# Third layer's end unrolled: attention parts first, norms behind them, inverses by node, skip rows made with K, V and Q

## The reference

```python
# third layer (H = 8 heads of DH = 16)
x_aug = concat([x, type_emb[node_types]], axis=-1)
K, Q, V = x_aug @ Wk, x_aug @ Wq, x_aug @ Wv
attn = einsum('ehd,ehd->eh', Q[dst], K[src]) * rel_scale[rel] / sqrt(DH)
attn_exp = exp(attn - max(attn))
attn_norm = attn_exp / (segment_sum(attn_exp, dst)[dst] + 1e-16)
out = segment_sum(attn_norm * V[src], dst) @ Wo + bo
h = out + x_aug @ Wskip
h = elu((h - mean(h)) * rsqrt(var(h) + 1e-5) * gamma + beta)
x = layernorm(x + h)
# fourth layer, its first part
C = 0.5 * (cos(edge_weight * pi / 10) + 1)          # one number per edge, the cutoff
W = (ssp(edge_attr @ mlp_w1.T + mlp_b1) @ mlp_w2.T + mlp_b2) * C
msg = (x @ lin1_w.T)[src] * W
```

## Time and profile before

| | |
|---|---|
| median of 3 runs | 9314.26 us (9308.85 to 9314.34) |
| profiled execution, its time | 9289.43 us |
| its span | 9287.6 us |
| busy: GpSimd, TensorE, VectorE, ScalarE | 66%, 57%, 53%, 19% |
| from the end of the third layer's loop to the first gather of the fourth | 6652.74 to 7105.95 us |

### The profile page before, as it was taken

One profiled execution on the slowest core, in us unless ns is written; L12 is line 12 of the kernel. 1 busy time (PEld: TensorE's weight loads), 2 busy tenths in 40 slices (PEclk: granted clock), 3 DMA queues, 4 the chain that ended last, 5 costly groups with the idle time before them and its releaser, 6 DMA issues. The chain is left out here.

```text
span 9287.6 us, 88604 instructions
## 1 busy us (share of the span) xinstructions
PE 5336.4 (57%) x27633; PEld 4325.2 (47%) x27633; DVE 4895.6 (53%) x10581; ACT 1745.2 (19%) x2599; POOL 6125.4 (66%) x6479
## 2 busy tenths in 40 slices
PE   4555555553344444444466666666435888887884
PEld 3444444442233333333355555555423555555553
DVE  5666666656422222222477777777654554555555
ACT  0000000002100000000300000000013555555553
POOL 5777777770377777777277777777403777777772
PEclk6666666665555555555677777777656878888886
DMA  5433434430233333333255555555301222222221
GB/s 172 115 114 111 115 110 115 113 105 2 57 77 77 75 77 76 75 77 75 84 166 164 164 165 164 164 164 164 91 1 52 73 74 74 72 74 72 74 73 36
DMA packets 391598, 906.48 MB, mean 98 GB/s; under 512 B 134405, under 2 KB 202936, under 8 KB 368288
## 3 DMA queue, kind: packets, MB, share of 16 engines
q0 software_dynamic: 232704, 538.22, 22.7%
q1 hardware_dynamic: 153538, 351.59, 12.6%
q10 hardware_dynamic: 4896, 11.01, 0.3%
HBM read 867.89 MB, written 32.45 MB: 97 GB/s over the span
## 5 line engine op out<-in xcount | busy, mean ns | idle before, releaser
L2117 POOL DMA_INDIRECT TMP<-schnet_table,src_idx x1616 | 1535.3, 950 | 964.1 <-issue 491.9
L1631 POOL DMA_INDIRECT PM<-hgt_kv_table,src_idx x1616 | 1528.0, 946 | 640.5 <-issue 467.0
L634 POOL DMA_INDIRECT PM<-gat_table,src_idx x1616 | 1531.8, 948 | 546.1 <-issue 492.2
L1177 POOL DMA_INDIRECT PM<-gcn_table,src_idx x1004 | 950.6, 947 | 306.0 <-issue 304.4
L1177 POOL DMA_INDIRECT TMP<-gcn_table,src_idx x612 | 577.3, 943 | 550.5 <-POOLq L1038 364.3
L1205 PE MATMUL ps<-TMP,PM 128*128 128x128 f32 x2008 | 515.5, 438 | 702.5 <-DMA PM<-gcn_table,src_idx 702.3
L1252 DVE TENSOR_TENSOR AC<-AC,ps 128x128 f32 x101 | 29.1, 288 | 1522.2 <-PE ps L1205 1522.2
L679 PE MATMUL ps<-PM 128*128 128x139 f32 x3232 | 781.2, 433 | 66.8 <-DVE PM L773 66.5
L1205 PEld LDWEIGHTS ps<-TMP,PM 128*128 128x128 f32 x2008 | 443.7, 325 | 763.8 <-DMA PM<-gcn_table,src_idx 626.9
L679 PEld LDWEIGHTS ps<-PM 128*128 128x128 f32 x3232 | 739.4, 327 | 73.1 <-DVE PM L773 72.8
L2144 PE MATMUL ps<-PM 128*128 128x128 f32 x3232 | 542.4, 321 | 362.6 <-issue 206.3
(11 more groups left out here) (383 smaller groups left out, 9008.2 us busy)
## 6 DMA issues: line engine op xcount, KB each, us to landing
PM<-local_dst_row SPq DMA_DIRECT2D x101, 1024.0 KB
PM<-local_dst_row SPq DMA_DIRECT2D x202, 512.0 KB, 3.9
PM<-in_attrT SPq DMA_DIRECT2D x101, 400.0 KB
xT<-in_rel_row SPq DMA_DIRECT2D x101, 384.0 KB, 4.8
PM<-gat_table,src_idx POOLq DMA_INDIRECT x1616
PM<-hgt_kv_table,src_idx POOLq DMA_INDIRECT x1616, 3.0
TMP<-schnet_table,src_idx POOLq DMA_INDIRECT x1616, 2.5
PM<-gcn_table,src_idx POOLq DMA_INDIRECT x1004, 2.5
```

Source lines behind the costliest of these rows:

```text
L634: pool.indirect_dma_start(out=g[:, par, t, 0:TAB0], out_offset=None, in_=tab0_d, in_offset=bass.IndirectOffsetOnAxis(ap=src_idx[:, i * ROU ...
L1177: pool.indirect_dma_start(out=g[n % DEEP][:, k, :], out_offset=None, in_=tab1_d, in_offset=bass.IndirectOffsetOnAxis(ap=src_idx[:, n * KT ...
L1631: pool.indirect_dma_start(out=g[:, par, t, 0:2 * P], out_offset=None, in_=kv_d, in_offset=bass.IndirectOffsetOnAxis(ap=src_idx[:, i * ROUN ...
L2117: pool.indirect_dma_start(out=g[:, b, k, :], out_offset=None, in_=tab3_d, in_offset=bass.IndirectOffsetOnAxis(ap=src_idx[:, (i * SLOTS + b ...
```

## The change

Second layer's loop: the type table for the skip part joins those of K, V, Q (t8, T8b now 512 columns wide), with the output bias added; one more load. Second layer's end: products 512 columns wide; the last 128, the skip rows, are copied by node into `skip`, which lies in xT. Third layer's loop: SP issues ten loads for what comes after, ahead of its own. Third layer's end: the rolled loop and the two blocks behind it become one unrolled block in BATCHES. The sums by head and the reference are turned to nodes, the inverse is taken by node (8 numbers), spread by ScalarE, turned back and multiplied in; products with output weights; skip rows added. This is done for all batches, then the norms follow. The cutoff is made on GpSimd as 1 - sin^2 with Sin on ScalarE; the row table is made group by group. Lines that are only moved are left out.

```diff
-        T8b = WA[0:TY, 0:3 * P // 2].bitcast(BF16)
+        T8b = WA[0:TY, 0:2 * P].bitcast(BF16)
...
+                sp.dma_start(out_bias, a["L2_gnn_bo"].partition_broadcast(NTYPE)).then_inc(hp_ld, 16)
...
-                    s.mark(dve.tensor_copy(T8s, PS[3][0:NTYPE, 0, 3 * P:4 * P]))
-                    s.link(dve.tensor_copy(t8, PS[3][0:NTYPE, 0, 0:3 * P]))
+                    s.mark(dve.tensor_copy(t8[:, 0:3 * P], PS[3][0:NTYPE, 0, 0:3 * P]))
+                    s.link(dve.tensor_tensor(t8[:, 3 * P:4 * P], PS[3][0:NTYPE, 0, 3 * P:4 * P], out_bias, ALU.add))
...
-                        nc.tensor.matmul(ps, xT[:, t_ * P:(t_ + 1) * P], WB[:, 0:3 * P], start=True, stop=False, skip_group_check=True)
+                        nc.tensor.matmul(ps, xT[:, t_ * P:(t_ + 1) * P], WB[:, 0:4 * P], start=True, stop=False, skip_group_check=True)
...
+                            nc.scalar.copy(skip[:, t_, :], PS[2 + t_ % 4 // 2][:, t_ % 2, 3 * P:4 * P]).then_inc(ev_act, 1)
...
+                            dve.tensor_copy(skip[:, t_, :], PS[2 + t_ % 4 // 2][:, t_ % 2, 3 * P:4 * P]).then_inc(ev_dve, 1)
...
+                for dst_, src_ in ((gamma, row_bc("L2_gnn_gamma")), (beta, row_bc("L2_gnn_beta")), (lin1, a["L3_gnn_lin1_w_T"]), (w1, a["L3_gnn_mlp_w1_T"]),
+                                   (w2, a["L3_gnn_mlp_w2_T"]), (lin2, a["L3_gnn_lin2_w_T"]), (linw, a["L3_gnn_lin_w_T"]), (b1, col_in("L3_gnn_mlp_b1")),
+                                   (l2b, col_in("L3_gnn_lin2_b")), (brow, a["L3_gnn_mlp_b2"].rearrange("(o f) -> o f", o=1))):
+                    sp.dma_start(dst_, src_).then_inc(late, 16)
                 either(sp, program)
+                sp.wait_ge(late, 160)
...
+            @block.gpsimd
+            def _(pool):
+                s = Steps(pool, cd)
+                pool.wait_ge(w_ld, 16)
+                s.link(pool.tensor_scalar(wk, cw, 0.05, None, ALU.mult))
+                s.link(pool.tensor_copy(wq, wk))
+                s.link(pool.tensor_scalar(wq, wq, -20.0, None, ALU.mult))
+                s.link(pool.tensor_tensor(wq, wq, cw, ALU.add))
+                pool.wait_ge(cs, 1)
+                s.link(pool.tensor_tensor(wq, wq, wq, ALU.mult))
+                s.link(pool.tensor_scalar(cw, wq, -1.0, 1.0, ALU.mult, ALU.add))
...
+                def turn_inverse(n):
+                    pe.wait_ge(wide, n + 1)
+                    if n >= 2:
+                        pe.wait_ge(num_ready, n - 1)
+                    for k, t_ in enumerate(tiles_of(n)):
+                        m = nc.tensor.transpose(group_ps(4 + n % 2, n)[:, k, :], y[:, t_, :], ident[:, :])
+                    m.then_inc(turned_r, 1)
+                def products(n):
+                    pe.wait_ge(num_ready, n + 1)
...
+                    for k, t_ in enumerate(tiles_of(n)):
+                        m = nc.tensor.matmul(group_ps(6 + n % 2, n)[:, k, :], acc2[:, 0, t_ * P:(t_ + 1) * P], WB[:, 4 * P:5 * P], start=True, stop=True)
+                    m.then_inc(out_mm, 1)
...
+                act.wait_ge(aged, 5)
+                nc.scalar.activation(age, age, ACT.Exp).then_inc(age_exp, 1)
+                for j in range(3):
+                    spread_inverse(j)
+                for j in range(3):
+                    rstds(j, 0)
+                exps(0)
+                exps(1)
+                rstds(0, 1)
+                norm(0)
+                finish(*BATCHES[0])
+                act.wait_ge(cd, 4)
+                nc.scalar.activation(wq, wq, ACT.Sin, scale=float(np.pi) / 20).then_inc(cs, 1)
+                exps(2)
+                rstds(1, 1)
+                norm(1)
+                finish(*BATCHES[1])
+                rstds(2, 1)
+                norm(2)
+                finish(*BATCHES[2])
...
+                def attended(j):
+                    def numerators(n):
+                        dve.wait_ge(turned_r, n + 1)
+                        num = acc2[:, 0, columns_of(n)].rearrange("p (k f) -> p k f", f=P)
+                        dve.tensor_tensor(num, num, group_ps(4 + n % 2, n), ALU.mult).then_inc(num_ready, 1)
+                    def with_skip(n):
+                        at = nodes_of(n)
+                        dve.wait_ge(out_mm, n + 1)
+                        dve.wait_ge(wide, BATCHES[j][1])
+                        dve.tensor_tensor(t[:, at, :], group_ps(6 + n % 2, n), skip[:, at, :], ALU.add).then_inc(out_read, 1)
+                    def stats(n):
+                        dve.wait_ge(out_read, n + 1)
+                        for t_ in tiles_of(n):
+                            s.mark(dve.bn_stats(out=st[:, t_, :], in_=t[:, t_, :]))
+                    lo, hi = BATCHES[j]
+                    for n in range(lo, hi + 2):
+                        if n < hi:
+                            numerators(n)
+                        if lo <= n - 1 < hi:
+                            with_skip(n - 1)
+                        if n - 2 >= lo:
+                            stats(n - 2)
+                    s.settle()
+                    variance(dve, s, st, w, span_of(BATCHES[j]))
+                    dve.sem_inc(var_ready[0], 1)
...
+                for j in range(3):
+                    inverses(j)
+                filter_bias()
+                attended(0)
+                attended(1)
+                attended(2)
+                first_norm(0)
+                first_norm(1)
+                residual(0)
+                first_norm(2)
+                residual(1)
+                scales(0)
+                residual(2)
+                scales(1)
+                scales(2)
```

More of the change, by code:

```diff
@@ new lines, in build, with sums_t @@
+        A = Arena(TMP, 0, TW)
+        cw = A.take(T)
+        after_cw = A.at
+        wq, wk = A.take(T), A.take(T, dtype=I32)
+        st = A.take(NT, 6)
+        w = {k: A.take(NT) for k in ("diff", "var", "mean2", "rstd", "shift")}
+        age = A.take(NT)
+        rz = asd
+        t = PM[:, 0:NP].rearrange("p (t f) -> p t f", f=P)
+        y = PM[:, NP:2 * NP].rearrange("p (t f) -> p t f", f=P)
+        ZB = 13
+        ZW = 33
+        reference = ref_b[:, (NR - 1) % 2, 0:1]
+        def sums_t(k):
+            lo, hi = k * ZB, min(k * ZB + ZB, NT)
+            return slice(lo, hi), PS[k // 2][:, k % 2, 0:(hi - lo) * ZW].rearrange("p (t z) -> p t z", z=ZW)
@@ new lines, in rstds, with exps @@
+                def rstds(j, k):
+                    at = span_of(BATCHES[j])
+                    act.wait_ge(var_ready[k], j + 1)
+                    nc.scalar.activation(w["rstd"][:, at], w["var"][:, at], ACT.Ln).then_inc(rstd_ln[k], 1)
+                    act.wait_ge(rstd_ln[k], j + 1)
+                    nc.scalar.activation(w["rstd"][:, at], w["rstd"][:, at], ACT.Exp, scale=-0.5).then_inc(rstd_ready[k], 1)
+                def exps(j):
+                    for n in range(*BATCHES[j]):
+                        act.wait_ge(y_ready, n + 1)
+                        nc.scalar.activation(t[:, nodes_of(n), :], y[:, nodes_of(n), :], ACT.Relu, scale=-1.0).then_inc(elu_ln, 1)
+                    for n in range(*BATCHES[j]):
+                        act.wait_ge(elu_ln, n + 1)
+                        nc.scalar.activation(t[:, nodes_of(n), :], t[:, nodes_of(n), :], ACT.Exp, scale=-1.0).then_inc(elu_ready, 1)
@@ new lines, in norm, with keep_x, keep_rows @@
+                def norm(j):
+                    act.wait_ge(scaled, j + 1)
+                    for t_ in tiles_in(BATCHES[j]):
+                        nc.scalar.activation(xn[:, t_, :], t[:, t_, :], ACT.Identity, scale=w["rstd"][:, t_:t_ + 1], bias=w["shift"][:, t_:t_ + 1]).then_inc(normed, 1)
+                def keep_x(n):
+                    act.wait_ge(x_t, n + 1)
+                    nc.scalar.copy(skip[:, nodes_of(n), :], group_ps(n % 2, n)).then_inc(x_copied, 1)
+                def keep_rows(n):
+                    act.wait_ge(row_mm, n + 1)
+                    nc.scalar.copy(y[:, nodes_of(n), :], group_ps(2 + n % 2, n)).then_inc(row_copied, 1)
@@ new lines, in finish @@
+                def finish(lo, hi):
+                    keep_x(lo)
+                    for n in range(lo, hi):
+                        if n + 1 < hi:
+                            keep_x(n + 1)
+                        keep_rows(n)
+                act.wait_ge(aged, 5)
[5 more added lines that the diff above has]
+                exps(0)
@@ new lines, in residual @@
+                def residual(j):
+                    for n in range(*BATCHES[j]):
+                        at = nodes_of(n)
+                        dve.wait_ge(elu_ready, n + 1)
+                        s.mark(dve.scalar_tensor_tensor(t[:, at, :], t[:, at, :], -1.0, xn[:, at, :], ALU.add, ALU.add))
+                    s.settle()
+                    for n in range(*BATCHES[j]):
+                        at = nodes_of(n)
+                        s.mark(dve.scalar_tensor_tensor(t[:, at, :], y[:, at, :], 0.0, t[:, at, :], ALU.max, ALU.add))
+                    s.settle()
+                    for t_ in tiles_in(BATCHES[j]):
```

(24 more changed lines are left out.)

296 lines of the change are left out of this document (106 added, 190 removed).

## The result

The changed kernel takes **9052.03 us** (median of 4 runs, 9050.59 to 9053.26); the kernel before, beside it, 9312.82 (4 runs, 9308.85 to 9314.34). The ratio is 0.9721, 95% interval 0.9704 to 0.9737. The forecast was 9058. The profiled execution took 9053.26 us with a span of 9051.3. One thing has to be known for the times further down: while e9, e5, e6, e8, e4 and e10 to e12 were measured, the four gather loops of every kernel, the kernel before too, took 1970 to 2240 us longer together, why isn't known, and so each run has beside it the time that the kernel before took along with it.

A forecast was written before the change was run, and what follows sets the result against it. Four gather loops, some 8080 of 9287.6 us, bound it, plus 453.2 us between third and fourth loop where nothing overlaps. Profiled 9289.43, −272 + 16, makes 9033.4; from the 9314.26 median, 9058; 8-in-10 range 9036 to 9086.

The forecast's parts named there:

- 2. attention: Third layer's end: attention parts in 12.5 groups of four tiles, 32 to 41 us by TensorE's clock level, 36 taken.
- 5. scales(2) done: Third layer's end: after norm(1), finish(1), rstds(2), scales(2) at 158.3 us; then norm(2), finish(2), first gather at 181.
- second layer's end: 50 tiles get products 512 columns wide, not 384; +16 us on the path, ends 13.5 and 27.
- price list: Operation times from the 141.9 us stretch between second and third loop, already written the new way, used to price the change.
- steps 3 and 4: Third layer's end: VectorE's norms and residuals to 105.5 us; then ScalarE's norm(0), finish(0), Sin, exps(2), VectorE's scales(1) to 139.
- 23 us wait: Third layer's end: VectorE idles some 23 us before residual(2), as ScalarE's order puts norm(0), finish(0), Sin before exps(2).
- the reciprocals: Old third layer's end: reciprocals of per-head sums spread to 128 rows, 41.6 us, among the largest single pieces removed.
- skip product: Old third layer's end: the per-tile product with the skip weights, 31.7 us, among the pieces removed.
- late loads: Ten loads SP issues ahead of the third loop's own: zero cost, 2 us to spare; 5.6 without cover.
- Step 1: Start of third layer's end: VectorE starts at 10.4 us, then short operations, reciprocals, filter bias; attention starts at 20.
- GpSimd slows VectorE: Rival, chance 0.10: GpSimd's four operations double VectorE's 9 us of short steps at the third layer's end; 9067 us.
- all low and all high: TensorE clock bounds for the third layer's end stretch: 194 us all low, 168 all high; each rival 0.12.

The follow-up runs named there:

- e9: Changed kernel, unchanged, run again as the measure for its group; stretch 181.2 us, median 11307.46 us, kernel before beside it 11544.94.
- e5: Changed kernel with VectorE doing attention, norms and scales batch by batch; stretch 159.3 us, median 11269.63 us, kernel before beside it 11544.94.
- e6: Changed kernel with products 384 wide, no skip copies, skip product in third layer's end, type rows and output bias omitted; stretch 189.6, median 11295.53 us (before 11544.94).
- e8: Changed kernel with staggered VectorE and ScalarE orders, filter bias last, GpSimd's arithmetic held back; stretch 149.3 us, median 11253.37 us (kernel before 11544.94).
- e4: Changed kernel without inverses by node: VectorE takes reciprocals of 128x512 per group; stretch 218.6 us, median 11061.56 us, kernel before beside it 11278.86.
- e10: e6 measured once more, same change against the changed kernel; stretch 189.8 us, median 11023.02 us, kernel before beside it 11278.86.
- e12: e8 with row copies of batches 1 and 2 on VectorE behind the filter bias; stretch 145.1 us, median 10981.68 us, kernel before beside it 11278.86.
- e3: Changed kernel with ScalarE doing Sin, third batch's exponentials and second batch's root ahead of the first norm and finish; stretch 163.8 us, median 9027.87 us.
- e7: Changed kernel with the ten late loads issued at the start of the third layer's end; stretch 180.0 us, median 9045.52 us.
- e2: Changed kernel with GpSimd's four operations held back until the first numerators are ready; stretch 176.5 us, median 9038.39 us.
- the table's first five rows: The changed kernel (9052.03 us), the kernel before profiled again (9308.01), e2, e3 and e7.

## Why the prediction was right

The forecast of each term of the schedule, with the clock from the last loop work, against the trace after:

| step | forecast | measured |
|---|---|---|
| 1. VectorE starts | 10.4 | 8.9 |
| attention starts | 20 | 24.4 |
| 2. attention | 36 (32 to 41) | 36.4 |
| 3. first norm to scales(0) | 49.5 | 49.3 |
| 4. norm(0), finish(0) | 15.3 | 14.8 |
| Sin and exps(2) | 9.3 | 9.0 |
| VectorE's wait | 23 | 22.06 |
| 5. scales(2) done | 158.3 | 163.0 |
| first gather | 181 | 182.3 |
| second layer's end | +16 | +14.5 |

**Right, with its mechanism.** The price list from the second layer's end held: steps 3 and 4 are the same operations at the same pitch, and came out within 1% and 4%. The 23 us wait was read from ScalarE's written order, and e3 moves it. The large term of what goes, the reciprocals, is shown by e4: 37 us. For the skip product, which had 31.7 us in the old chunks, e6 and e10 show 8.5 in the new schedule. No run takes back the rest of the 271 us, the rolled chunks and the separate blocks; that part is read from the busy and idle times above, and from e3, e5 and e8, where the same work takes 18 to 32 us less by its order alone. The second layer's end grew by 14.2 to 14.5, tiles of 512 columns following at 1.08 us when the level is high:

```profile
4556.31 1.02 PE L1407 MATMUL ps<-WB,xT 128*128 128x512 f32 x2
4557.17 0.38 PE L1408 MATMUL ps<-WA,PM 72*128 72x512 bf16 x1
4557.39 1.02 PE L1407 MATMUL ps<-WB,xT 128*128 128x512 f32 x2
```

The late loads were put at zero in the third loop, and e7 shows zero.

**A rival that came true inside the forecast.** Step 1 said 9.6 us from VectorE's start to attention; it took 15.5. The rival *GpSimd slows VectorE* had a chance of 0.10 and a price of 9 us; e2 shows it to be the cause and its price 5.8. Its form was wrong: not all short steps twice as long, but three of them standing still, and those with a PSUM operand not at all. The three are casts and a tensor_scalar; operations with two inputs from SBUF, which the prediction names, are lengthened in e3, e5 and e8. GpSimd's own four operations were sized well, 15 us forecast and 13.8 measured. That the sum stayed right in spite of it was luck: other terms were set too high, by 4.8 together: the start (1.5), finish(2) (10.5 forecast, 7.9 measured) and the way to the first gather (5.0 and 4.3).

**Clock.** The middle was taken between all low and all high, and attention came out in the middle: each batch starts at the low level and ends at the high one (four transposes take 1.06 us at first and 0.60 later). e12 shows that the same code can be 4 us shorter when the level rises earlier, and attention took 34.1 us in e7, so a spread around 36 is real; no run came to either bound, 32 or 41.

**Table loads.** In the trace after, an activation follows its load by 0.01 us and the next load follows the activation by 0.02:

```profile
6816.71 1.28 ACT L2007 ACT_TABLE_LOAD   x1
6818.00 0.22 ACT L2007 ACTIVATE TMP<-TMP 128x16 f32<-128x16 f32 x1
6818.24 1.28 ACT L2009 ACT_TABLE_LOAD   x1
```

The drain that the Trainium skill, ScalarE: Activation LUTs, "What ACT_TABLE_LOAD costs", adds to a switch isn't there, and leaving it out was right.

**What the medians add.** They differ by 260.8 us, 4.4 more than the two stretches give. The fourth loop differs by more than that between executions of the same code (2026.5 and 2046.3 us). The forecast added to its 9033.4 for a profiled execution the 25 us by which the first profile lay under its median. They belong to that one execution: in the changed kernel the profiled run and the median are 1.2 us apart, and the forecast of 9033.4 is 20 us under the profiled 9053.26, because its loops weren't at 2020 each but at 2023 to 2031. What carries over is the difference between two medians; that it comes within 5 us of the two stretches says that the loops took about the same time in the other runs of both kernels, which no profile shows. What makes the loop longer in some runs wasn't tried.

## What to carry to other kernels

Where engines take turns, price the new code from a stretch written the same way, and follow each engine's written order: a wait that the order makes (22 us here) can be read before it is measured. Doing one phase for all batches first isn't overlap in itself; it separates the phases, and here batch by batch is 22 us and a staggered order 32 us faster with the same work. An elementwise operation on GpSimd isn't free because GpSimd is idle: what VectorE has beside it decides, and that changes with each change of order. Work that is moved to an earlier stage is only free if that stage has room: the skip rows were put where TensorE was already the bound.

## What the runs showed of the hardware

- Some VectorE operations on SBUF alone stand still while GpSimd's elementwise operation runs, however small they are: a cast of 128 elements took 3.50 us and ended 0.08 us after GpSimd. It took the 128x50 tensor_scalar, the casts of 1x512 and 1x128, and operations with two SBUF inputs (two 128x128 passes of 2.85 and 1.69 us in e3, 128x16 ones of 1.71 and 1.39 in e5). Tensor_scalar on 128x1 (0.15 us), memsets, statistics, reciprocals (3.25 us for three, with and without GpSimd beside them) and operations with a PSUM operand ran on. In e2 four 128x16 operations with two SBUF inputs also ran on, at 0.18 us, beside GpSimd's 4.28 us multiplication; what is different there isn't known.
- GpSimd waits for VectorE as well: its square took 3.91 us in e3, where VectorE's passes had begun first, and 2.88 in the changed kernel.
- GpSimd takes 4.30 us for a multiplication by a constant on 128x1616, 1.53 for a conversion from integers, 3.64 for a sum of two and 2.88 for a square. A multiplication and a sum with two constants in one operation takes 1.54, less than the multiplication alone (4.30 and 4.29).
- The same 1616 gathers with the same median of 944 ns (947 in the profile after) spanned 2026.5 to 2046.3 us in the six profiles of the table's first five rows and of before; the share of gathers over 0.98 us differs, from 97 to 263 of them.
- In attention the level rose at different times in runs of the same code: a mean of 0.95 in the first 9.5 us in one, 0.76 in the first 13.2 in another, where the two levels are 0.50 and 1.00.
